# Constant fp32 products in free PSUM banks, ahead of the first slot and behind the first untangling and turning of each slot

## What is computed

```
x = x + tanh(g_xattn[l]) * xattn_l(layernorm(x), ctx)
x = x + tanh(g_ffn[l])   * ffn_l(layernorm(x))
```

```
qh, kh, vh = split_heads(q @ wq + bq), split_heads(k @ wk + bk), split_heads(v @ wv + bv)
probs = softmax(einsum('bhqd,bhkd->bhqk', qh, kh) / sqrt(HEAD_DIM))
out = einsum('bhqk,bhkd->bhqd', probs, vh).transpose(0, 2, 1, 3).reshape(B, -1, D) @ wo + bo
```

## Time and profile before

| | us |
|---|---|
| median of three runs | 1383.23 |
| the profiled execution, its own time | 1382.49 |
| its span, first to last instruction | 1380.7 |
| PE busy in the span (88%) | 1218.4 |
| DVE busy (51%) | 702.7 |
| ACT busy (32%) | 448.5 |
| the slots, first `weigh` to the last projection | about 425 to 757 |
| mean granted clock of TensorE | 0.918 |

### The profile page before, as it was taken

How to read it: one execution, slowest core, us unless ns; L and a number is a source line. 1 busy time by engine, 2 the same in 40 slices (tenths; PEclk the granted TensorE clock), 3 DMA queues, 4 the chain that set the end, 5 groups by cost and what they waited for, 6 DMA issues and landing times.

```text
span 1380.7 us, 19327 instructions
## 1 busy us (share of the span) xinstructions
PE 1218.4 (88%) x6360; PEld 766.8 (56%) x6361; DVE 702.7 (51%) x1997; ACT 448.5 (32%) x842; POOL 292.9 (21%) x347
## 2 busy tenths in 40 slices
PE   6999999999978899999988759999756699999993
PEld 4534434434443444454443649999655556788862
DVE  7273365366984556545652531111176753455557
ACT  3322132223353455444434103333233200333320
POOL 2111111040121111001000041111122564255660
PEclk9999999999988999999998669999977789999997
DMA  9999999100000000000100845555309322455538
GB/s 300 338 338 333 334 334 320 47 31 0 1 1 1 1 1 1 1 1 1 34 1 1 257 145 188 187 183 170 121 20 347 130 92 92 136 168 161 170 112 312
DMA packets 140488, 186.75 MB, mean 135 GB/s; under 512 B 8736, under 2 KB 124960, under 8 KB 140288
## 3 DMA queue, kind: packets, MB, share of 16 engines
q1 hardware_dynamic: 130864, 159.28, 37.3%
q0 software_dynamic: 9552, 26.52, 5.2%
HBM read 83.71 MB, written 102.06 MB: 135 GB/s over the span
## 4 chain that ended last, share of the span: by engine, by line
PE 75%; DVE 12%; ACT 4%; DMA 3%; issue 3%; POOL 2%; SPq 1%; POOLq 0%; DVEq 0%; ACTq 0%
PE psum L2003 14%; PE psum L1266 6%; PE psum L1277 6%; PE psum L2215 5%; PE psum L1055 5%; PE psum L1074 3%; PE psum L936 2%; PE psum L2272 2%; PE psum L2249 2%; PE psum L2296 2%; PE psum L1996 2%; PE psum L2031 2%; PE psum L2193 2%; DVE arena L2834 2%; PE psum L947 2%
## 5 line engine op out<-in xcount | busy, mean ns | idle before, releaser
L2003 PE MATMUL psum<-arena 128*128 128x512 f32 x432 | 204.1, 623 | 0.0
L2834 DVE TENSOR_REDUCE arena<-psum 128x4 f32<-128x616 f32 x128 | 101.6, 797 | 99.2 <-PE psum L2215 98.0
L2003 PEld LDWEIGHTS psum<-arena 128*128 128x128 f32 x432 | 82.4, 197 | 118.5 <-issue 117.7
L2215 PE MATMUL psum<-arena 32*128 32x308 f32 x512 | 105.4, 504 | 16.6 <-DVE arena L2834 15.7
L1182 POOL DMA_INDIRECT ys<-xnT,arena x96 | 92.1, 959 | 91.7 <-DVE xnT L1159 69.1
L2416 ACT ACTIVATE arena<-psum,arena 128x512 f32<-128x512 f32 x72 | 49.0, 685 | 172.8 <-PE psum L2003 163.1
L1894 POOL TENSOR_TENSOR x_tok<-x_tok,add_row 128x1024 f32<-128x1024 f32 x16 | 38.3, 2400 | 269.3 <-ACT xn L1759 269.2
L2507 ACT ACTIVATE arena<-psum 128x2048 f32<-128x2048 f32 x40 | 75.0, 1874 | 59.6 <-PE psum L2253 42.6
L1055 PE MATMUL psum<-arena,xn 128*128 x384 | 87.1, 380 | 2.3 <-ACT xn L1105 1.9
L1266 PEld LDWEIGHTS psum<-side,arena 128*128 128x128 f32 x736 | 87.4, 195 | 2.7 <-ACT side L1311 1.6
L1266 PE MATMUL psum<-side,arena 128*128 128x128 f32 x736 | 87.9, 279 | 1.0 <-ACT side L1311 1.0
(11 more groups left out here) (418 smaller groups left out, 2092.4 us busy)
## 6 DMA issues: line engine op xcount, KB each, us to landing
xs<-zeros SPq DMA_DIRECT2D x8, 8576.0 KB, 60.2
arena<-in_W SPq DMA_DIRECT2D x31, 1024.0 KB, 5.0
xn<-xs SPq DMA_DIRECT2D x64, 134.0 KB, 2.3
arena<-in_gate_up SPq DMA_DIRECT2D x4, 2048.0 KB, 15.7
arena<-xs SPq DMA_DIRECT2D x32, 134.0 KB, 2.4
arena<-in_down SPq DMA_DIRECT2D x4, 1024.0 KB, 14.6
arena<-ys SPq DMA_DIRECT2D x4, 1024.0 KB, 12.7
arena<-ys SPq DMA_DIRECT2D x2, 2048.0 KB, 14.1
```

The lines of the kernel that those rows point to most:

```text
L2003: ins = pe.matmul(bank[dict(hn=4, r=5, z=6, xn=7)[k]][:], lhs[:, cols], r, start=(start and n == 0), stop=(stop and n == len(w) - 1))
L2215: ins = pe.matmul(bank[most_bank(n, k) + i][:, 0:2 * M].rearrange("p (h m) -> p h m", h=2), qhT[rows, n % 3, c, t * P:(t + 1) * P], keys[r ...
L2834: dve.tensor_reduce(neg[:, n % 2, t, 2 * pair:2 * pair + 2, 2 * c:2 * c + 2], psum[:, most_bank(n, k):most_bank(n, k) + 2, 0:2 * M].rearra ...
```

## The change

Two things are added to `flow()` and one function to PE's part. `hold(n, many)` issues `many` products of the constant `ones` (128x128, fp32) with the constant `ident` (128x128, fp32) into 128 columns of bank 2 and bank 3 in turn. Nothing reads what they write; the next `weigh` writes these banks anew. With n = -1 it waits for what `weigh(0, 4)` waits for too (x_done of step 1, second group); otherwise it waits until the exponential of `weigh(n, 2)` is done, `weighed` at 5n + 4, the count for which `weigh(n, 3)` waits too. ACT, DVE and POOL skip the new operation. There are 12 products ahead of `shift(0)`, and in each of the slots 0 to 6 two behind `untangle(n, 0)` and three behind `turn(n + 2, 0)` (slot 6 has no turn there): 12 + 7 x 5 = 47 products.

```
@@ flow
             for k in range(16):
                 yield ("most", 0, k)
                 yield from after.get(k, ())
+            yield ("hold", -1, 12)
             yield ("shift", 0)
@@ slot
+            def held(many):
+                return [("hold", n, many)] if n + 1 < SLOTS else []
...
             yield ("weigh", n, 2)
             yield from most()
             yield ("untangle", n, 0)
+            yield from held(2)
             yield from most()
             yield from itertools.islice(second, 1)
             yield from ahead("turn", n + 2, 0)
+            yield from held(3)
             yield from most()
             yield ("untangle", n, 1)
             yield from ahead("turn", n + 2, 1)
@@ mha_tensor
+            def hold(n, many):
+
+                if n < 0:
+                    pe.wait_ge(*x_done.at(1, 2))
+                else:
+                    pe.wait_ge(weighed, weighed_at[n, 2] + 1)
+                for k in range(many):
+                    pe.matmul(bank[2 + k % 2][:, 0:P], ones[:], ident[:], start=True, stop=True)
```

More of the change, by code:

```diff
@@ L2343, in mha_tensor @@
                 elif op[0] not in ("tanh", "settle", "normalise", "norm1", "norm2"):
-                    dict(late_turn=late_turn, late_product=late_product, first=first, second=second, turn=turn, query=query, most=most, shift=shift, weigh=weigh, rests=rests, values=values,
+                    dict(late_turn=late_turn, late_product=late_product, first=first, second=second, turn=turn, query=query, most=most, hold=hold, shift=shift, weigh=weigh, rests=rests, values=values,
                          untangle=untangle, back=back, project=project, tri_turn=tri_turn, tri=tri)[op[0]](*op[1:])
@@ L2539, in mha_scalar @@
                     normalise_scalar(act, int(op[0][4]), op[1])
-                elif op[0] not in ("most", "untangle", "project", "tri", "settle", "rests", "finish", "product", "late_product"):
+                elif op[0] not in ("most", "untangle", "project", "tri", "settle", "rests", "finish", "product", "late_product", "hold"):
                     dict(late_turn=late_turn, first=first, second=second, turn=turn, query=query, shift=shift, weigh=weigh, values=values, back=back, tri_turn=tri_turn,
```

## The result

The changed kernel is slower: 1401.69 us in the median of nine runs, against 1382.4 us in nine runs of the kernel before; the ratio is 1.0114, 95% interval 1.0085 to 1.0143. The forecast was 1389.7, slower by 0.5%, with a range up to 1397. The direction is right; the size is not, and the time lies outside the range.

What follows compares the result with a forecast made beforehand. TensorE was taken to bound the kernel. Terms: -3.3 (first stretch), +11.5 (waits), -1.1 (absorbed), -0.6 (clock in later slots) = +6.5 on 1382.49, so 1389.0, or 1389.7 on the median's footing; range 1381 to 1397.

Steps and rivals of the forecast that it cites:

- The bound: Whole kernel: TensorE (PE) bounds, busy 88% of the span; a microsecond its queue stands still in a slot is generally lost.
- The price of a product: Each added product: 0.24 us at full clock, two 0.48, three 0.72, twelve 2.87; up to twice that at half clock.
- the twelve are hidden: Ahead of slot 0: the wait for GpSimd hides the twelve products; without that cover they would cost 2.87 us.
- Their gain of 3.3 us: Slot 0's start, turning to weighing r = 0: full clock makes 9.72 us into 6.4, 3.3 us back.
- upper bound of 4.9: Same place at slot 0's start: about 4.9 us back if the 9.19 us busy simply halved.
- The wait for the exponential: Slots 0 to 6: PE waits until r = 2's exponential leaves the banks; +11.5 us together.
- what is absorbed: Slots: 1.1 us off the +11.5, since PE stands idle some 2.7 us of each slot's 45 elsewhere.
- The clock in slots 1 to 6: Half-clock stretches there: +1.4 us for slot 1, -1.0 for each of the two long ones, sum -0.6.
- The last one: Rival: gate closes more often, first stretch stays, slots 0 and 4 get one, long ones not shortened; 1398.4 us, chance 0.17.
- The first rival: The clock holds in slots 1 to 6 and the wait is paid: -0.1, so 1383.1 us; chance 0.20.

Runs made afterwards that it cites:

- e8: e4 with the three products behind the turning again, the change's waits for the exponential kept, and filler products ahead of each wait; ratio 1.0003 to the kernel before.
- e4: The change's 47 products, the slots' ones written to the next operation's bank without waiting for the exponential, three ahead of the turning; 0.9939 against the kernel before.
- e1: Only the twelve products ahead of slot 0, none in the slots, against the kernel before; ratio 0.9987.

## Why the prediction was wrong, step by step

**The bound** (PE, standing still is lost): right. The 13.3 us of waits put into PE's queue came back in the section as 13.7 us, before any loss of clock.

**The price of a product**, 0.24 us, and that the twelve are hidden: right (2.94 us for twelve). **Their gain of 3.3 us**: right for the stretch at hand, 9.72 to 6.15 us, but the clock fell 10 us later instead, and part of it was given back. The forecast had counted it as won. (Its upper bound of 4.9 does not follow from 9.19 us halved, which is 4.6; nothing hangs on it.)

**The wait for the exponential**: right in its place, its releaser and its length; 3.04, 3.69 and 1.44 us were expected as 3.0, 3.6 and 1.4, and only slot 6's 0.77 as hardly any. Its price was too low: +11.5 less 1.1 for what is absorbed, where e8 less e4 shows 13.7 at an equal clock. By slot (start of one slot's first exponential to the next's, e8 less e4) it is 2.95, 3.34, 1.67 four times and 0.75, against +2.4, +2.8, +1.5 and +0.3. Of the 3.3 us that are missing, 1.1 is what was taken off as absorbed and was not; the rest is 0.2 to 0.6 us a slot by which the queue behind the wait was followed too tightly. At full clock in the changed kernel itself slot 4 takes 45.12 us against 43.42, +1.7.

**The clock in slots 1 to 6**: this is the step that failed. The text took it that "as many stretches stay as now", and the two long ones get shorter, -0.6 us; with the -3.3 of the first that is -3.9 for the clock. Measured, from the turning of slot 0's maxima to the last exponential, the change takes 349.6 us against 328.9, so +20.7 in all (22.0 in the section, less 1.3 won ahead of it). Take off the 13.7 of the waits and +7.0 is left for the clock, where -3.9 was forecast: 10.9 of the 14.2 us by which the sum of +6.5 falls short, the other 3.3 being the price of the waits. The number of stretches did stay, at seven, but they did not get shorter: 6.8 us became the rule, 10.2 in slot 2, slot 5 had two, and they moved to places with dense work behind them (the products themselves, a context product, a turning). So the section has 51 us at half clock in place of 40, and each was dearer: going from before to e4 took away 19 us at half clock for 4.8 us of section, 0.25 for each with the products' own work in it, while the change's 31 us more than e8's cost 0.43 each. Where the clock held, in slots 3 and 4, the forecast's arithmetic fits to 0.2 us. The dense products did not make up for the idle time ahead of them; set against the kernel with the waits alone they go with 14 us less at half clock, but not with less than before the change, and in a stretch at half clock they took up to 1.2 us for two and 1.5 for three themselves.

**The rivals.** The last one, more stretches, at 1398.4 with a chance of 0.17, came nearest to 1401.69, though not by its own account: the first stretch did go. The first rival (the clock holds, the wait is paid: -0.1) is just what e8 shows, 1.0003. So the two effects had been seen one by one; what was wrong was to let them cancel in the likeliest case. The wait that the products bring is itself the idle time that they were to prevent, and it comes first in the queue. The Trainium skill, "TensorE: Matmul & The Clock Gate", in the table under "Why this matters for your kernels", warns of idle gaps between bursts of matmuls; this trace agrees, with the clock at 1.00 up to the end of a wait of 3.04 us and at 0.50 from the product behind it. Of the waits of 1.44 us, those in slots 2 and 5 had a fall within 1.4 us of their end, those in slots 3 and 4 had none; what decides between them is not shown. The page's Part 4, that transposes do not count as work the way products do, is not contradicted: with two and three products among the transposes and no wait (e4) the clock stays full in slots 1 to 5. But no kernel here had other transposes or none in that place, so whether it was the kind of work or the gaps filled is open.

What stays open: the difference of the medians in the result is 19 us and the ratio of 1.0114 makes 16, against 20.7 in one trace each. Where the stretches fall can differ from run to run, and one trace shows one case; only the mean clock of the other runs is on record.

## What to carry to other kernels

A filler that is to hold the clock must itself wait for nothing: choose its output bank by what is free at that point of the queue, not by what is unused in between, and write it where the next operation writes anyway, under that operation's wait. Put as much of it as the wait at hand is long (two or three products for waits of 0.3 to 0.9 us here), since most of what is more is paid; and fill all thin places of a section, as with a single one filled the clock fell at another: at 433 in place of 424 in the change, and in the later slots in e1. When a change brings both a wait and a remedy for waits, price the case in which the wait wins as the likeliest until a row says otherwise.

## What was not expected of the hardware

That sixty-one products which nobody reads make the kernel 1.15% faster: some 14 us of added work on PE, in time that it did not use, bought back 44 us at half clock, 40 of them in the section, which got 12.7 us shorter. In the change the time at half clock was dearer, 13.1 us for 31 us more than in e8, or 0.43 us for each. And that the spread of a single core's times is so wide: the part behind the slots, the same code in all kernels, took 627.7 to 647.4 us in the traces. Why is not looked into here.
